# Cross attention: context turned in 32x32 blocks on VectorE, scores in 32-row products

## The reference

```python
def _L0_xattn_ref(encoder_hc, decoder_hq, w_sim, b_sim, W_qv, b_qv):
    ...
    w1, w2, w3 = (w_sim[:d], w_sim[d:2 * d], w_sim[2 * d:])
    Sim = (encoder_hc @ w1)[:, :, None] + (decoder_hq @ w2)[:, None, :] + jnp.einsum('bid,bjd->bij', encoder_hc * w3, decoder_hq) + b_sim[0]
    A = jax.nn.softmax(Sim, axis=2)
    hq_hat = jnp.einsum('bij,bjd->bid', A, decoder_hq)
    Batt = jax.nn.softmax(jnp.max(Sim, axis=2), axis=1)
    hc_bar = jnp.einsum('bi,bid->bd', Batt, encoder_hc)[:, None, :]
    hc_hat = jnp.broadcast_to(hc_bar, encoder_hc.shape)
    feats = jnp.concatenate([encoder_hc, hq_hat, encoder_hc * hq_hat, encoder_hc * hc_hat], axis=-1)
    hcq = feats @ W_qv + b_qv
    return hcq
...
x = x + _L0_xattn_ref(_layernorm(x, axis=-1), ctx_1024, ...)
```

## Time and profile before

| | |
|---|---|
| median of 3 runs | 1582.35 us (1582.21 to 1584.47) |
| profiled execution, span | 1606.2 us (the profile gives no other time of that execution) |
| TensorE busy over the span | 1417.7 us, 88% |
| VectorE, ScalarE, GpSimd busy | 721.5, 377.6, 756.1 us |
| cross attention | from 0 to about 842 us |

### The profile page before, as it was taken

The page is one execution under the profiler, slowest core; times in us unless marked ns, Lnnn a source line. Parts: engine busy times, 40 slices in busy tenths (PEclk is TensorE's granted clock), DMA queues, the critical chain, the costliest instruction groups (busy, mean ns, idle before and its releaser), DMA issues. The chain is left out here.

```text
span 1606.2 us, 28597 instructions
## 1 busy us (share of the span) xinstructions
PE 1417.7 (88%) x9329; PEld 914.6 (57%) x9330; DVE 721.5 (45%) x1715; ACT 377.6 (24%) x716; POOL 756.1 (47%) x592
## 2 busy tenths in 40 slices
PE   5899999999999999999998777898549999996960
PEld 3455555555555555555546556666438888885750
DVE  2443434434344344443437776787583233231221
ACT  1322222322223222232215412222301111111110
POOL 0134431444214442144406855787495886806830
PEclk9999999999999999999998999999679999998985
DMA  9514542244422444224406569532103333314322
GB/s 331 191 53 147 177 177 92 107 154 176 172 96 99 162 176 161 107 92 169 170 7 224 165 242 318 176 111 97 66 27 131 137 137 131 139 57 144 117 67 103
DMA packets 94905, 225.10 MB, mean 140 GB/s; under 512 B 9448, under 2 KB 25960, under 8 KB 94864
## 3 DMA queue, kind: packets, MB, share of 16 engines
q1 hardware_dynamic: 85136, 191.02, 34.0%
q0 software_dynamic: 9200, 32.51, 5.8%
q10 hardware_dynamic: 528, 1.05, 0.2%
HBM read 179.20 MB, written 45.35 MB: 140 GB/s over the span
## 5 line engine op out<-in xcount | busy, mean ns | idle before, releaser
L487 DVE COPY ctxT<-T 128x512 f32<-128x512 f32 (+1 forms) x208 | 139.6, 671 | 251.4 <-PE T L353 251.4
L487 ACT COPY ctxT<-T 128x512 f32<-128x512 f32 (+1 forms) x208 | 118.7, 570 | 450.0 <-PE T L353 450.0
L390 PE MATMUL S<-ctxT,qT 128*64 128x384 f32 (+2 forms) x1280 | 211.7, 448 | 0.0
L318 POOL TENSOR_TENSOR xb<-x_sb,bqv_b 128x512 f32<-128x512 f32 x16 | 20.3, 1272 | 256.9 <-DMA x<-xb 256.9
L331 POOL TENSOR_TENSOR wb<-wb,x 128x2048 f32<-128x2048 f32 x30 | 135.5, 4538 | 0.0
L353 PEld LDWEIGHTS T<-ident,ctx_one 128*128 128x128 f32 (+1 forms) x896 | 92.0, 141 | 63.6 <-ACT ctxT L487 34.9
L315 POOL TENSOR_TENSOR rstd<-ve,mhalf 128x1 f32<-128x1 f32 x16 | 8.8, 551 | 252.7 <-DVE nmean L573 252.7
L353 PE MATMUL T<-ident,ctx_one 128*128 128x128 f32 (+1 forms) x896 | 116.9, 273 | 0.0
L327 POOL TENSOR_TENSOR wb<-w,hcb 128x2048 f32<-128x2048 f32 x30 | 107.5, 3606 | 19.1 <-DVE w12L L646 19.1
L1881 POOL TENSOR_TENSOR w_high<-w_low,f_zero 128x2048 fp32r<-128x2048 f32 x21 | 96.8, 4609 | 36.3 <-DMA w_low<-_L_ffn_gate_up_proj_dram 24.7
L1932 PE MATMUL f_Dn<-w_high,f_hH 128*128 x156 | 67.9, 435 | 49.6 <-issue 48.0
(11 more groups left out here) (299 smaller groups left out, 2925.0 us busy)
## 6 DMA issues: line engine op xcount, KB each, us to landing
x<-in_ctx_dram SPq DMA_DIRECT2D x32, 768.0 KB, 7.3
ctx_one<-in_ctx_dram SPq DMA_DIRECT2D x32, 768.0 KB, 5.6
ctx_two<-in_ctx_dram SPq DMA_DIRECT2D x32, 768.0 KB, 7.3
ctx_one<-in_ctx_dram SPq DMA_DIRECT2D x32, 512.0 KB, 5.4
w_low<-_L_ffn_gate_up_proj_dram POOLq DMA_DIRECT2D x10, 1024.0 KB, 8.3
f_xt<-routed_x SPq DMA_DIRECT2D x39, 256.0 KB
routed_y<-f_yt SPq DMA_DIRECT2D x39, 256.0 KB
ctx_one<-in_ctx_dram SPq DMA_DIRECT2D x32, 256.0 KB
```

The source lines that it names most:

```text
L390: last = pe.matmul(S[64 * b:64 * b + 64, k, col:col + w], qT[:, c, 64 * b:64 * b + 64], buf[:, b, c, 0:w], start=(c == 0), stop=(c == C - 1))
L487: copy(buf[:, bank, :, i * P:i * P + rows], T[bank][:].rearrange("p (c j) -> p c j", c=C)[:, :, 0:rows]).then_inc(t_free[bank], 1)
```

## The change

- The context is no longer turned on TensorE. VectorE's 32x32 block transpose (`turn_first`, `turn_second`, `turn_third`) writes ctxA and ctxB, so that partition 32a + r of feature block k holds feature 32k + r of the context rows of quarter a. `probs` now lies in ctxB's memory.
- `scores` has three blocks. Each is a sum over 16 feature blocks k, for four row groups a (32 rows of the array each) and two column groups b; row group a writes bank a of S. The 65-row tile is padded to 96 rows.
- The four row groups need q at all four partition quarters. ScalarE makes q in f3, stores it to a DRAM tensor (`q_d`, 256 KB) and loads it back four times, into `qr` (each 256 KB), all issued on ScalarE's own queue.
- The layer norm's last step moves from VectorE to ScalarE and one body earlier; GpSimd makes mean x rstd for it.
- The maximum is taken once, after all scores, over two banks at a time; five exponentials take four banks each, or a part of the last tile.
- TensorE's body: hc, all values, scores(0), hqh, scores(1), first half of the output product, scores(2), wb products and second half with the probs transposes.
- SP loads ctx_one in four parts, with x between the second and third; tiles 0 to 3 have two buffers, the other nine one. The loop has one body pair less.
- hqhH/L and f2H/L share one pair of buffers (hfH, hfL); two loads for the next stage are split.

```diff
-BLOCKS = [(0, 3, 0, 0), (3, 3, 1, 0), (6, 3, 2, 0), (9, 2, 3, 0), (11, 2, 3, 256)]
+BLOCKS = [(0, 4, 0), (4, 5, 8), (9, 4, 4)]
 NBLK = len(BLOCKS)
-BANK_TILES = [(0, 3), (3, 3), (6, 3), (9, 4)]
-TWO_SLOTS = 2
-AV_ORDER = [t for j in [*range(TWO_SLOTS, NBLK), *range(TWO_SLOTS)] for t in range(BLOCKS[j][0], BLOCKS[j][0] + BLOCKS[j][1])]
+TAIL_POS = 8
+AV_ORDER = [*range(4, 13), *range(0, 4)]
+PARTS_ONE = [(4, 2, False), (6, 2, True), (8, 2, False), (10, 2, False)]
+PART_ENDS = [1, 4, 6, 8]
 AT_TILES = [(0, 4), (4, 3), (7, 3), (10, 3)]
+EXPS = 5
+AT_AFTER = [1, 4, 5, 5]
+Q = 32
+QUADS = P // Q
...
-                    sp.wait_ge(av_one, (NBLK - TWO_SLOTS) * p + j - TWO_SLOTS + 1)
-                    load_block(j, None, nxt)
-                if store:
                     sp.wait_ge(x1_ready, p)
                     sp.dma_start(x1[prev], xb[1 - s][:]).then_inc(x1_out, 16)
+                for i in range(len(PARTS_ONE)):
+                    if i == 2 and load:
+                        sp.wait_ge(hc_ready, p + 2)
+                        sp.wait_ge(xb_ready, p + 2)
+                        load_x(after)
+                    sp.wait_ge(av_one, len(PARTS_ONE) * p + i + 1)
+                    load_part(i, nxt)
                 if load:
-                    sp.wait_ge(hc_ready, p + 2)
-                    sp.wait_ge(xb_ready, p + 2)
-                    load_x(ahead)
                     sp.wait_ge(av_done, p + 1)
-                    for j in range(TWO_SLOTS):
-                        load_block(j, s, ahead)
+                    load_two(s, after)
...
-            def scores(j, p, f, fs, loads, step):
-                t0, n, k, col = BLOCKS[j]
-                w = block_cols(j)
-                buf = ctxT[(j + fs) % 2]
-                for bank in range(2):
-                    pe.wait_ge(t_free[bank], turn(bank, f"ctx{j}.{2 * n - 2 + bank}", p, step) + 1)
+            def scores(j, f):
+                t0, n, col = BLOCKS[j]
+                buf = (ctxA, ctxB)[j % 2]
+                pe.wait_ge(turned[j], f + 1)
                 if j == 0:
-                    pe.wait_ge(q_ready, C * (f + 1))
-                    pe.wait_ge(exp_done, 4 * f)
-                for c in range(C):
-                    if j + 1 < NBLK and c < BLOCKS[j + 1][1]:
-                        turn_ctx(j + 1, 2 * c, p, fs, loads, step)
-                        turn_ctx(j + 1, 2 * c + 1, p, fs, loads, step)
-                    for b in range(2):
-                        last = pe.matmul(S[64 * b:64 * b + 64, k, col:col + w], qT[:, c, 64 * b:64 * b + 64],
-                                         buf[:, b, c, 0:w], start=(c == 0), stop=(c == C - 1))
+                    pe.wait_ge(q_in, 64 * (f + 1))
+                    pe.wait_ge(exp_done, EXPS * f)
+                for k in range(DB):
+                    c, e = k // QUADS, k % QUADS
+                    for a in range(QUADS):
+                        w = n * Q
+                        if t0 <= TAIL_POS < t0 + n:
+                            w += min(max(JTAIL - a * Q, 0), Q) - Q
+                        for b in range(2):
+                            last = pe.matmul(S[64 * b:64 * b + 64, a, col * Q:col * Q + w], qr[a * Q:(a + 1) * Q, e, c, 64 * b:64 * b + 64],
+                                             buf[a * Q:(a + 1) * Q, b, k, 0:w], start=(k == 0), stop=(k == DB - 1))
                 last.then_inc(qk_done, 1)
...
+            def values(p, s, step):
+                pe.wait_ge(hqh_ready, p)
+                for n, pos in enumerate(AV_ORDER):
+                    for q in range(len(AT_TILES)):
+                        if AT_TILES[q][0] == n:
+                            pe.wait_ge(t_free[q % 2], turn(q % 2, f"probs{q}", *before(p)) + 1)
                     if n == 1:
-                        if front:
-                            pe.wait_ge(hc_ready, f + 1)
-                            turn_tile(0, "hc", tok_rows, p, step)
-                        if back:
-                            pe.wait_ge(tcol_ready, p + 1)
-                            fill(1, "trow", p, step)
-                            pe.transpose(T[1][0:1, 0:P], tcol[:], ident[:]).then_inc(t_full[1], 1)
...
-                        src, i = context(s, b, t)
-                        last = pe.matmul(O[64 * b:64 * b + 64, :], probsT[0:rows, t, 64 * b:64 * b + 64],
+                        pe.wait_ge(tcol_ready, p + 1)
+                        fill(1, "trow", p, step)
+                        pe.transpose(T[1][0:1, 0:P], tcol[:], ident[:]).then_inc(t_full[1], 1)
+                    for b in range(2):
+                        rows = tile_rows(pos)
+                        src, i = context(s, b, pos)
+                        last = pe.matmul(O[64 * b:64 * b + 64, :], probsT[0:rows, n, 64 * b:64 * b + 64],
                                          src[0:rows, i, :], start=(n == 0), stop=(n == JT - 1))
-                    if back and n == (10 if front else 4):
+                    if n in PART_ENDS:
+                        last.then_inc(av_one, 1)
+                    if n == 5:
                         pe.wait_ge(x1_ready, p)
                         pe.wait_ge(brow_ready, p + 1)
                         pe.matmul(Y[:, 0:P], ones1[:], brow[:], start=True, stop=True).then_inc(brow_full, 1)
-                    if back and t in [t0 + n - 1 for t0, n, _, _ in BLOCKS[TWO_SLOTS:]]:
-                        last.then_inc(av_one, 1)
+                last.then_inc(av_done, 1)
...
-                    scores(0, p, f, fs, loads, step)
-                    for j in range(1, NBLK - 1):
-                        scores(j, p, f, fs, loads, step)
+                    scores(0, f)
                 if back:
                     pe.wait_ge(hqh_ready, p + 1)
                     turn_tile(0, "hqh", tok_rows, p, step)
                 if front:
-                    scores(NBLK - 1, p, f, fs, loads, step)
+                    scores(1, f)
                 if back:
...
-                        if front and c >= 2:
-                            turn_probs(c - 2, p, step)
+                        if front and c == 3:
+                            turn_probs(0, p, step)
                         for b in range(2):
                             pe.matmul(Y[64 * b:64 * b + 64, :], hcT[s][:, c, 64 * b:64 * b + 64], wb[:, b, c, :],
                                       start=False, stop=False)
-                    pe.wait_ge(t_free[0], turn(0, "hqh", p, step) + 1)
+                    pe.wait_ge(f2L_ready, p + 1)
                     for c in range(C):
-                        if front and c < 2:
-                            turn_probs(2 + c, p, step)
...
+            def norm(f):
+                act.wait_ge(nr_ready, f + 1)
+                act.activation(tok_rows[:], x_sb[:], ACT.Identity, scale=rstd[:, 0:1], bias=nr[:, 0:1]).then_inc(hc_ready, 1)
...
+                        act.activation(f3[:, c, :], hcT[fs][:, c, :], ACT.Identity, scale=w3T[:, c:c + 1],
+                                       bias=w2T[:, c:c + 1]).then_inc(q_made, 1)
+                    act.wait_ge(q_made, C * (f + 1))
+                    if later(f, 1):
+                        act.wait_ge(q_in, 64 * f)
+                    act.dma_start(q_d, f3[:].rearrange("p c i -> p (c i)")).then_inc(q_out, 16)
+                    act.wait_ge(q_out, 16 * (f + 1))
+                    if later(f, 1):
+                        act.wait_ge(qk_done, NBLK * f)
+                    for a in range(QUADS):
+                        act.dma_start(qr[a * Q:(a + 1) * Q].rearrange("p e c i -> p e (c i)"),
+                                      q_d.rearrange("(e r) d -> r e d", r=Q)).then_inc(q_in, 16)
                 if back:
                     act.wait_ge(av_done, p + 1)
                     act.wait_ge(rz_ready, p + 1)
                     if front:
...
-            steps(act, body)
...
+                    def exp(i, a0, a1, pos, col, n, w):
+                        act.activation(probs4[:, a0:a1, pos:pos + n, 0:w], S4[:, a0:a1, col:col + n, 0:w], ACT.Exp, bias=nmx[:, 0:1],
+                                       accum_out=z5[:, i:i + 1]).then_inc(exp_done, 1)
...
+                    full = JTAIL // Q
+                    exp(0, 0, QUADS, 4, 8, 4, Q)
+                    exp(1, 0, full, TAIL_POS, JT - 1, 1, Q)
+                    exp(2, full, full + 1, TAIL_POS, JT - 1, 1, JTAIL % Q)
+                    exp(3, 0, QUADS, TAIL_POS + 1, 4, 4, Q)
+                    exp(4, 0, QUADS, 0, 0, 4, Q)
+                    drain_probs(act, copy, 1, p, step)
+                    drain_probs(act, copy, 3, p, step)
...
+            def turn_two(buf, src, i, b, col):
+                return dve.transpose(buf[:, b, :, col * Q:(col + 2) * Q].rearrange("p k (t r) -> p t k r", r=Q),
+                                     src[:, i:i + 2, :].rearrange("p t (k r) -> p t k r", r=Q))
...
+            def turn_second(f):
+                dve.wait_ge(ctx_one_in[0], 16 * part_dmas(0) * (f + 1))
+                for b in range(2):
```

(19 more changed lines are left out.)

410 lines of the change are left out of this document (196 added, 214 removed).

## The result

| | before | after |
|---|---|---|
| median of the runs, us | 1582.28 (1582.12 to 1584.47) | 1716.93 (1715.38 to 1721.04) |
| profiled execution, span, us | 1606.2 | 1714.3 |
| first and last exponentials of the attention, us | 49.0 and 805.7 | 64.6 and 947.4 |
| period of a pair of batches, us | 50.4 | 58.85 |

After takes 1.0859 times as long as before (interval 1.084 to 1.0878): slower, where 1427 us and faster was forecast. Both ends of the attention agree with that: its first body ends 15.6 us later than before and each of 15 more takes 8.4 us longer, 142 us. The sum from 1582 would be 1724, 7 us above the median measured. Where these 7 us went isn't shown: the profiled execution of before was itself 24 us above its median, and not in the attention.

The account below looks back on a forecast made before the run. TensorE, busy 99.97 of 100 us, bounds the kernel. Period 36.1 + 2.1 + 0.9 + 0.8 + 0.6 = 40.5 us instead of 50.4; 15 bodies save 149 us, the first 7: 1582.35 becomes 1427 us. Range 1380 to 1575, chance 0.82.

Parts of the forecast that it names:

- The q trip: Storing q and loading it four times before scores(0): TensorE waits 2.1 us a pair, from 0 to 7.
- read-in at half share of 410 GB/s: q's four loads beside ctx_one's parts: 1 MB takes 5.2 us plus 1.8, landing at 15.2 us.
- Instruction fetch: TensorE's loop of about 3540 instructions: fetching might add 16 us in all, giving 1443; left out of the forecast.
- score blocks: Scores as 768 recorded products in rounds of eight, all groups overlapping: 11.1 us a pair, against 10.7 before.
- Clock: Half clock on TensorE after the wait before scores(0): 0.6 us a pair, from 0 to 3.
- First body: The attention's first body, its scores running between transposes from 25.2 to 48 us: ends perhaps 7 us sooner.
- row groups do not overlap: Rival on the score products: the four row groups run in turn, scores 44.4 us, period 73.8, 1926 us; chance 0.14.
- loads limit the rounds: Rival on the score rounds: sending or weight loads bind, scores 19.2 to 20.5 us, 1548 to 1568 us; chance 0.13.
- The transposes: Context turned on VectorE: twelve instructions at 1.29 us and two at 0.73, together 16.9 us a pair, hidden.
- late q or a colder clock: Rival before scores(0): q lands at 20 us or waits halve the clock; period 46, 1509 us; chance 0.16.
- transposes at half rate: Rival on VectorE: context transposes take 31 us, turned parts come late; period 51, 1584 us; chance 0.04.
- turned by 16.7 and needed at 19.4: VectorE's second context block: ready at 16.7 us of the body, needed by its scores at 19.4.

Follow-up runs that it names:

- parts_late: The change, with SP issuing all of the next pair's ctx_one parts and ctx_two only after q has landed; 1659.7 us.
- q_once: The change, with q made, stored and loaded back for the first pair alone, all later scores using that q; 1556.22 us, ratio 0.9835.
- q_pe: The change, with q spread to the four partition quarters by 16 TensorE products and four copies instead of through memory; 1581.34 us, ratio 0.9991.
- k4: q_once with only 4 of the 16 feature blocks in the scores; 1364.3 us.
- before_long: The kernel before, with four pairs in TensorE's loop instead of two, same instructions in the same order; 1582.10 us, ratio 1.0002.
- q_pe_wide2: q_pe with second and third score blocks merged and the normed rows' transposes sent in the middle of the first block; 1527.83 us, ratio 0.9677.

## Why the prediction was wrong

*The q trip: wrong, the largest error.* The forecast had q stored by 8.2 us and loaded by 15.2 after the start of the body, a wait of 2.1, with 7 as its upper end. In the body shown the four activations are done 4.4 us after the first transpose (4.0 by the sum), the store lands at 497.2, 10.0 us after it, and the loads at 514.9, 27.7. The step that failed is "read-in at half share of 410 GB/s", from which the wait of 2.1 us follows: 1 MB in 17.6 us is 60 GB/s, a fifth of what was moved and not a half. In those 17.7 us 4.56 MB go by the other queue, q1, for 1.05 MB of q on q10, and the engines are full (queues, 497.2 to 514.9 us; slices of 1.5 us, 484 to 544 us):

```profile
q1 hardware_dynamic: 1153, 4.56, 82.7%
q10 hardware_dynamic: 576, 1.05, 20.8%
```
```profile
DMA  0004289999999999999994000000000000000000
GB/s 11 0 11 175 30 287 315 374 386 310 299 356 292 299 296 302 315 321 321 321 415 180 11 11 0 0 11 0 11 0 11 0 0 11 0 0 0 0 0 11
```

Two errors lie in it: q's share, and an upper end taken as if only ctx_one's 4.3 MB stood beside it, at 410 GB/s, when the stretch moves about 315. The row that gave 5.8 us for 256 KB behind other transfers was of one transfer, not of four in a row. The wait measured 14.3 us (143.1 in ten). This step alone turns the sign: 40.5 and 12.2 more is 52.7 us a pair, above the 50.4 of before. parts_late shows that it is the sharing: with the context held back the loads land in 4.4 us.

*Instruction fetch: put at nothing, and it decides once the trip is gone.* The earlier trace rows had one packet in 100 us, and the estimate of 16 us in all stood in a sentence by itself. Even that would have been far too low, since it took one transfer for each branch, and a loop fetched whole is some sixteen packets a pass (67 in 8.4 pairs of q_once). Measured are gaps of 3.3 us a pair in the change, about 50 us in all, and of 6.5 in q_once, about 98. A bound from rows was to be had: nothing in the trace of before shows a loop of 3,540 instructions, and so the cost had to be open above. In q_once, where the trip no longer covers it, score blocks that were to take 11.1 us take 20.7; in the change itself they take 18.7 (5.96, 6.36 and 6.39). Of these 7.6 us too many, 3.3 are gaps and 1.9 half clock behind the wait for q; the other 2.4 are rounds a little slower than the sum.

*The sum of the misses.* With those two, the body shown is longer than the forecast's by 12.8 us of q and 7.6 of scores, 20.4; the period is longer by 18.4, since 0.6 us of clock were in the sum already and the rest of the body is 1.4 us shorter than summed.

*Clock.* 0.6 us a pair, from 0 to 3: the mechanism of the earlier trace rows holds. The first block takes 1.9 us more than the third, which is inside the range.

*First body.* To end 7 us sooner; it ends 15.6 later. Its scores wait for the same trip and then for instructions: the gaps in them are 8.2 us. q_pe, without the trip, ends it 9 us sooner than the change.

*What held.* All eight groups run beside each other: 256 products of 128 columns take 3.87 us in q_once, less the last one's 0.27 that is 0.113 us a round of eight, for 0.107 by the sum. So the rivals "row groups do not overlap" and "loads limit the rounds" are out. By "TensorE: Matmul & The Clock Gate", Back-to-back issue gap, of the Trainium skill 256 products would take 6.4 us, an estimate at its 25 ns; the trace differs, 14 ns each, so the floor of 25 ns does not hold across groups. The transposes take 1.21 us for 1.29 and 0.66 for 0.73. The maximum is done 2.4 us after the last score (2.6), and the gap before the probs transposes is 0.6 us (0.9). Taking the context transposes off TensorE did bring what was said: the body without scores and without the wait for q is 25.3 us, for 26.7 by the sum.

*The rivals.* The one that came true is the first, "late q or a colder clock", at three times its price: the period is 18.4 us over the forecast, where it had 5.5. None of the rivals had the fetch. The two that I let end on the slow side, no overlap of rows and transposes at half rate, had the wrong mechanism. The 0.82 of the range also counts the 0.02 that would have ended above 1575. k4 says how far even the sum without trip and fetch was off: from 40.5, less the q wait (2.1) and the 12 blocks left out (8.3), comes 30.1, where 36.1 was measured and 35.1 with s1 moved. Of the 5.0 us that stay, the wait for the second turned part is 2.3 (25.7 in eleven), that for the third 1.0 in the body shown, and half clock behind the first of them, an estimate, 1 to 1.5; "turned by 16.7 and needed at 19.4" was too kind to VectorE, which first stands for s1 and then for ctx_one. The last 0.2 to 0.7 us stay open. Open also is where exactly the step of the held loop lies, and whether a held loop with all 768 records would give the forecast period; no run has one.

## What to carry to other kernels

Count the instructions of a loop as well as their time: many short products beside each other are worth their rate only if the loop is held, or if its instructions are used up more slowly than they come in (before_long). An instruction queue that moves nothing in a tuned loop is a resource in use, not a line without meaning. Price a transfer on the critical path by all that the other queues move in that stretch, and when two costs may cover each other, take the larger away first and expect the other to appear.

## What the runs showed of the hardware that was not expected

- TensorE's instructions came in packets of 16 KB; a loop of about 1,430 was held, one of about 1,620 was not. With dense short products a packet's worth of 256 lasts 1.9 us, packets begin some 3.5 us apart, and gaps of up to 3.4 us (q_once) and 4.2 us (q_pe_wide2) end 2.2 to 2.9 us after a packet began.
- A loop that is fetched anew but uses its instructions at 13 a microsecond loses nothing that can be measured (ratio 1.0002, before_long).
- VectorE's multiply with a sum over 512 elements takes 0.69 us alone and 4.06 us when GpSimd runs its 2048-column product beside it; the 32x32 transposes beside the same work keep their 1.20 us.
- Four loads of 256 KB on one queue, beside 4.6 MB on another, got 60 of some 317 GB/s; with that queue held back they landed in 4.4 us.
